# Two integer weight matrices handed to the kernel as bf16 instead of int32, read by the same casting-queue DMAs

## The chip, the cores and the metric

The kernel runs on 8 cores of one Trainium2 chip, one sequence of 2048 tokens on each core; no core exchanges anything with another. The metric is the time on the device of the slowest core, in microseconds (us).

## The reference, cut to what matters

```python
# x: (8, 2048, 1024); xn: layer norm of x
def _dequant(q, scales, g):            # q: integers 0..255, one scale per 128 rows and column
    K, N = q.shape
    w = (q.astype(float32) - 128.0).reshape(K // g, g, N) * scales[:, None, :]
    return w.reshape(K, N)
# layer 0, FFN
w1 = _dequant(fc1_q, fc1_scales, 128)  # fc1_q: int (1024, 4096)
y  = silu(h @ w1 + fc1_bias)
w2 = _dequant(fc2_q, fc2_scales, 128)  # fc2_q: int (4096, 1024)
z  = y @ w2 + fc2_bias
x  = x + attention0(xn) + (xn + 0.5 * z)
# layer 1: x = x + causal attention (16 heads) + FFN with values rounded to a small float format
```

The softmax of layer 0's attention runs over an axis of length one, so that attention is a sum of the values over all tokens and costs little. The change touches fc1_q and fc2_q alone.

## The kernel before, in words

The tokens of a core stay in SBUF as `X` (8 MB, f32). The program is a row of phases, each written as blocks for each engine; semaphores order the engines, and each instruction of VectorE and ScalarE waits for the one before on its engine (class `_Chained`, lines 56 to 97, so most rows carry L97 of that helper, and their waits L78).

The phases in order:

1. `_ph_loads` and `_ph_consts`: SP loads `X` and eight small tables (CON, a table of constants, is the last); VectorE makes constants once all of them are there.
2. `_ph_w1_dequant` (L430 to L464), eight rounds, one for each 128 rows g of fc1. POOL's queue loads `QIB` (128x4096, bf16 in SBUF) from `fc1q` (L439); ACT's queue loads `SCB` (128x2048 f32, one row broadcast to 128 partitions, 1 MB) for each half of the columns. For each half VectorE computes (QIB - 128) * SCB into `WB`, the whole of w1 in bf16 (8 MB). There is one QIB and one SCB: the next QIB is issued when both halves of the round are through (semaphore sDQ), the next SCB when the half before it is.
3. `_ph_w2_dequant_spill` (L467 to L514), 32 tiles of 128 rows of fc2. POOL's queue loads QIB (128x1024, two places used in turn) from `fc2q` (L480), ACT's queue loads SCB (128x1024 f32, 512 KB), VectorE computes the product into `WQB` (one place, 256 KB), and POOL's queue stores WQB to `w2sp` in HBM (L485). Product g waits for QIB g, SCB g and for the store of tile g-1 to have landed. When product g-1 is done, three DMAs go out: SCB g on ACT's queue, then on POOL's the store of tile g-1 and the load of QIB g+1, which is not needed until one tile later.
4. `_ph_ln` (layer norm statistics), `_ph_xsum_a0` (layer 0's attention), `_ph_ffn` for layer 0 with WB held and w2 streamed from `w2sp`; within it the tiles of layer 1's w2 are rounded on VectorE and stored to `wqsp`. Then the same for layer 1 (w1 loaded by `_ph_w1_load_l1`), the attention of layer 1, the projection and the store of `X`.

VectorE takes the phases in program order: the layer norm of phase 4 begins on it only when the products of phases 2 and 3 are through, and TensorE's first matmul waits for the layer norm's first pass.

QIB is a bf16 tile in SBUF. The sources are declared at L118 and L120 and prepared on the host at L1464 and L1466:

```python
c.fc1q = dram("fc1q", [D, FF], I32)
e.dma_start(out=c.QIB[:, :], in_=c.fc1q[128 * g:128 * (g + 1), :])     # L439
e.dma_start(out=c.QIB[:, D * (g % 2):D * (g % 2) + D],                 # L480
            in_=c.fc2q[128 * g:128 * (g + 1), :])
```

so these DMAs read 4 bytes an element, cast, and write 2. A row of fc1q is 16 KB in HBM and 8 KB in SBUF, a row of fc2q 4 KB and 2 KB.

Of the kernel before, what the change touches and what calls it, by code (L numbers as in the profile page):

```python
# [9 lines left out]
BF16 = mybir.dt.bfloat16  # L10
I32 = mybir.dt.int32
# [5 lines left out]
D = 1024  # L17
T = 2048
FF = 4096
# [86 lines left out]
def build_nc(stop="full"):  # L106
    _INC_REC.clear()
    _SEM_TOT.clear()
    nc = bass.Bass("TRN2", target_bir_lowering=False)
    c = Ctx()  # L110
    c.nc = nc
    c.stop = stop

    dram = lambda n, sh, ty, kind="ExternalInput": nc.dram_tensor(n, sh, ty, kind=kind).ap()
    c.x = dram("x", [128, NCH * T], F32)
    c.wvt = dram("wvt", [D, D], F32)
    c.wot = dram("wot", [D, D], F32)
    c.fc1q = dram("fc1q", [D, FF], I32)  # L118
    c.fc1sb = dram("fc1sb", [1, 8 * FF], F32)
    c.fc2q = dram("fc2q", [FF, D], I32)  # L120
    c.fc2sb = dram("fc2sb", [1, 32 * D], F32)
    c.gam = dram("gam", [128, NCH], F32)
    c.bet = dram("bet", [128, NCH], F32)
    c.f1b = dram("f1b", [128, NFO], F32)
    c.f2b = dram("f2b", [128, NCH], F32)
    c.qkvt = dram("qkvt", [D, 3 * D], F32)
    c.projt = dram("projt", [D, D], F32)
    c.bpj = dram("bpj", [128, NCH], F32)
    c.w1t = dram("w1t", [D, FF], F32)
    c.b1l1 = dram("b1l1", [128, NFO], F32)  # L130
    c.w2t = dram("w2t", [FF, D], F32)
    c.b2l1 = dram("b2l1", [128, NCH], F32)
    c.cvec = dram("cvec", [128, 8], F32)
    c.m4 = dram("m4", [128, 4 * TSW], BF16)
    c.out = dram("out", [128, NCH * T], F32, "ExternalOutput")
    c.w2sp = dram("w2sp", [FF, D], BF16, "Internal")
    c.wqsp = dram("wqsp", [FF, D], BF16, "Internal")
    c.rowsp = dram("rowsp", [4, T], F32, "Internal")
    c.rowspb = dram("rowspb", [1, D], BF16, "Internal")
    c.qksp = dram("qksp", [128, 2 * NCH * T], BF16, "Internal")  # L140
    c.f1sp = dram("f1sp", [128, NCH * T], F32, "Internal")

    with contextlib.ExitStack() as es:
        _body(c, es)
    return nc
# [1305 lines left out]
def host_prep(L0_attn_x, L0_attn_w_qkv, L0_attn_w_o, L0_ffn_ln_gamma,  # L1451
              L0_ffn_ln_beta, L0_ffn_fc1_q, L0_ffn_fc1_scales, L0_ffn_fc1_bias,
              L0_ffn_fc2_q, L0_ffn_fc2_scales, L0_ffn_fc2_bias, L1_attn_w_qkv,
              L1_attn_w_proj, L1_attn_b_proj, L1_ffn_w1, L1_ffn_b1, L1_ffn_w2,
              L1_ffn_b2):
    import ml_dtypes
    A = lambda v: np.ascontiguousarray(v)
    f32 = np.float32
    cm = lambda vec, k: A(np.asarray(vec, f32).reshape(k, 128).T)

    sh = {}
    sh["wvt"] = A(np.asarray(L0_attn_w_qkv, f32)[2048:3072, :].T)
    sh["wot"] = A(np.asarray(L0_attn_w_o, f32).T)
    sh["fc1q"] = A(np.asarray(L0_ffn_fc1_q, np.int32))  # L1464
    sh["fc1sb"] = A(np.asarray(L0_ffn_fc1_scales, f32).reshape(1, 8 * FF))
    sh["fc2q"] = A(np.asarray(L0_ffn_fc2_q, np.int32))  # L1466
    sh["fc2sb"] = A(np.asarray(L0_ffn_fc2_scales, f32).reshape(1, 32 * D))
    sh["gam"] = cm(L0_ffn_ln_gamma, NCH)
    sh["bet"] = cm(L0_ffn_ln_beta, NCH)
    sh["f1b"] = cm(L0_ffn_fc1_bias, NFO)  # L1470
    sh["f2b"] = cm(L0_ffn_fc2_bias, NCH)
    wq = np.asarray(L1_attn_w_qkv, f32)
    qkv = np.concatenate([wq[:, 0:64, :].reshape(NH * 64, D),
                          wq[:, 64:128, :].reshape(NH * 64, D),
                          wq[:, 128:192, :].reshape(NH * 64, D)], axis=0)
    sh["qkvt"] = A(qkv.T)
    sh["projt"] = A(np.asarray(L1_attn_w_proj, f32).T)
    sh["bpj"] = cm(L1_attn_b_proj, NCH)
    sh["w1t"] = A(np.asarray(L1_ffn_w1, f32).T)
    sh["b1l1"] = cm(L1_ffn_b1, NFO)  # L1480
    sh["w2t"] = A(np.asarray(L1_ffn_w2, f32).T)
    sh["b2l1"] = cm(L1_ffn_b2, NCH)
    cvec = np.zeros((128, 8), f32)
    cvec[:, 0] = 0.5 + 2.0 ** -20
    cvec[:, 1] = EPS
    sh["cvec"] = cvec
    p = np.arange(128)[:, None]
    qq = np.arange(TSW)[None, :]
    sh["m4"] = A(np.concatenate([(qq >= 128 * r + p) for r in range(4)],
                                axis=1).astype(ml_dtypes.bfloat16))  # L1490
    x = np.asarray(L0_attn_x, f32)
    in_maps = []
    for b in range(x.shape[0]):
        m = dict(sh)
        m["x"] = A(x[b].T.reshape(NCH, 128, T).transpose(1, 0, 2
                                                         ).reshape(128, NCH * T))
        in_maps.append(m)
    return in_maps
# [21 lines left out]
```

How the kernel before makes its waits and increments, by code:

```python
    def wait_ge(self, sem, val):  # L65
        return self._eng.wait_ge(sem, val)
# [1 line left out]
    def _edge(self):  # L68
        if self._prev is None:
            return
        rec = _INC_REC.get(id(self._prev))
        if rec is None or rec[1] is not self._seq:
            if rec is None:
                tgt = self._prev
            elif self._nop is not None:
                tgt = self._nop(self._eng)
            else:
                tgt = self._eng.engine_nop()
            _rec_then_inc(tgt, self._seq, 1)
            rec = _INC_REC[id(tgt)]
        self._eng.wait_ge(rec[1], rec[2])
# [287 lines left out]
    @blk.vector  # L369
    def _(e):
        e.wait_ge(c.sINd.h, c.sINd.v)
        e.wait_ge(c.sME.h, 1)
        e.tensor_scalar(out=c.CON[:, 2:3], in0=c.CON[:, 0:1], scalar1=C52,
                        scalar2=C52, op0=ALU.add, op1=ALU.subtract)
# [25 lines left out]
    @blk.gpsimd  # L400
    def _(e):
        for g in range(34):
            if g >= 2:
                e.wait_ge(c.sWQ.h, wq0 + g - 1)
            if g < 32:
                sb_ = c.sSPe if g % 2 == 0 else c.sSPo
                e.dma_start(out=c.SCW[:, 1024 * (g % 2):1024 * (g % 2) + D],
                            in_=c.w2t[128 * g:128 * (g + 1), :]
                            ).then_inc(sb_.h, 16); sb_.v += 16
            if g >= 2:
                e.dma_start(out=c.wqsp[128 * (g - 2):128 * (g - 1), :],
                            in_=c.WQB[:, :]
                            ).then_inc(c.sWQd.h, 16); c.sWQd.v += 16
# [860 lines left out]
    @blk.tensor  # L1274
    def _(e):
        e.wait_ge(c.sVTe.h, c.sVTe.v)
```

## Time and profile before

| | us |
|---|---|
| median of two runs | 4875.44 (4867.91 and 4882.96) |
| the profiled execution, its own time | 4875.03 |
| its span on the slowest core (core 7) | 4873.5 |
| spans of all cores | 4840.0 to 4873.5 |

The profiled execution's own time is 1.5 us more than its span, from the first to the last instruction. All cores show a mean granted TensorE clock of 0.669 to 0.672. The page names engines PE (TensorE), PEld (its weight loads), DVE (VectorE), ACT (ScalarE), POOL (GpSimd) and SP (SyncE); a "q" behind a name is its sequencer or queue. A DMA's bytes are counted as it writes them, so a load of QIB counts 1 MB or 256 KB whatever its source holds. DMA queues: q0 is POOL's, q10 ACT's, q1 SP's.

### The profile page before, as it was taken

Reading aid. Unit: us, or ns where it says so; the run is one execution under the profiler, and the core shown is the slowest. Engines: PE = TensorE matmul, PEld = TensorE weight load, DVE = VectorE, ACT = ScalarE, POOL = GpSimd, SP = SyncE. Lnnn points to the kernel's source line nnn. Section 1 sums busy time; section 2 is a strip of 40 time slices with the busy share of each in tenths; the row PEclk is TensorE's granted clock in tenths of the full one; section 3 lists DMA queues with packets and bytes.
Section 4 is the critical chain, followed back from the end, with each engine's and each line's share of the span. In section 5 each row is a group of like instructions: output and inputs, shape, how many; then the busy total and the mean of one; then the engine's idle time right before and its main releaser. Section 6 shows DMA issues by size and latency. Waiting matters only on the chain.

```text
span 4873.5 us, 25503 instructions; the slowest of 8 cores (4840.0 to 4873.5 us)
## 1 busy us (share of the span) xinstructions
PE 2228.2 (46%) x6689; PEld 726.5 (15%) x6689; DVE 1901.3 (39%) x2583; ACT 804.4 (17%) x1324; POOL 178.1 (4%) x336
## 2 busy tenths in 40 slices
PE   0002016384574246046145334423433577777775
PEld 0000002131231012012011111211110111111111
DVE  1213315555555373574466367333412111111113
ACT  0000003123130010010011011011000244444440
POOL 0010000000000000000000000000100000000001
PEclk9998558696886567566656765766755555555557
DMA  6563422231415202001100200223222100000005
GB/s 173 151 153 77 9 53 61 70 113 35 108 63 110 13 0 66 25 0 36 55 0 6 78 7 0 69 53 59 50 33 30 30 9 9 9 9 9 9 1 155
DMA packets 111755, 243.53 MB, mean 50 GB/s; under 512 B 31352, under 2 KB 35448, under 8 KB 107258
## 3 DMA queue, kind: packets, MB, share of 16 engines
q0 software_dynamic: 36112, 107.50, 9.8%
q1 hardware_dynamic: 57646, 85.12, 7.0%
q10 hardware_dynamic: 17856, 49.29, 4.3%
q8 instruction: 56, 0.92, 0.1%
q14 instruction: 85, 0.70, 0.1%
HBM read 243.89 MB, written 42.02 MB: 59 GB/s over the span
## 4 chain that ended last, share of the span: by engine, by line
DVE 37%; DMA 22%; PE 18%; ACT 10%; issue 9%; DVEq 2%; ACTq 0%; POOL 0%; SPq 0%; POOLq 0%
DVE SCR L97 26%; PE PS L1319 6%; ACT PT L97 6%; DVE YA L97 3%; PE PS L954 3%; DMA w2sp<-WQB 3%; DMA BCA<-rowsp 3%; DMA wqsp<-WQB 3%; PE PS L1298 2%; PE PS L1210 2%; DMA VW<-qkvt 2%; ACT SCR L97 2%; DMA W2B<-wqsp 2%; PE PS L1137 2%; DVE PT L97 2%
## 5 line engine op out<-in xcount | busy, mean ns | idle before, releaser
L890 PE MATMUL PS<-HBB,WB 128*128 128x512 bf16 x2048 | 668.2, 497 | 1081.0 <-DVE YA L97 429.2
L97 DVE TENSOR_TENSOR SCR<-SCR 128x512 f32<-128x512 f32 (+2 forms) x835 | 627.4, 751 | 442.3 <-DVEq L78 357.3
L954 PE MATMUL PS<-YA,W2B 128*128 128x512 bf16 x2048 | 469.6, 387 | 98.3 <-DVE YA L97 42.3
L890 PEld LDWEIGHTS PS<-HBB,WB 128*128 128x128 bf16 x2048 | 231.0, 117 | 1517.4 <-issue 1398.7
L200 ACT COPY CON<-CON 128x1 f32<-128x1 f32 x610 | 116.6, 191 | 1636.4 <-DVE YA L97 742.4
L1298 PE MATMUL PS<-PT,VT 128*65 128x512 bf16 x640 | 304.8, 631 | 143.4 <-DVE PT L97 143.4
L1319 PE MATMUL PS<-QKP 64*128 64x512 bf16 x640 | 299.3, 620 | 61.1 <-ACT PT L97 45.9
L97 DVE TENSOR_TENSOR SCR<-X,BCA 128x512 f32<-128x512 f32 x224 | 155.0, 692 | 404.1 <-DVEq L78 387.4
L97 ACT ACTIVATE PT<-PS 128x2048 bf16<-128x2048 f32 x160 | 300.4, 1877 | 14.8 <-ACT CON L200 0.5
L546 PE MATMUL PS<-YA,ONE 128*1 128x512 bf16 x64 | 39.3, 614 | 517.2 <-DVE YA L97 517.2
L954 PEld LDWEIGHTS PS<-YA,W2B 128*128 128x128 bf16 x2048 | 196.8, 99 | 372.8 <-issue 162.5
L1137 PE MATMUL PS<-XNS,QKW 128*128 128x512 bf16 x512 | 127.7, 416 | 249.9 <-DVEq L97 249.9
L97 DVE TENSOR_TENSOR PT<-PT,M 128x2048 bf16<-128x2048 bf16 x64 | 78.4, 1225 | 407.8 <-DVEq L78 405.9
L1210 PE MATMUL PS<-VW,XNS 128*128 128x512 bf16 x256 | 112.5, 618 | 201.9 <-DMA VW<-qkvt 129.0
L97 ACT ACT_TABLE_LOAD x10 | 12.8, 1283 | 1121.2 <-DVE STAT L97 498.0
L200 ACT ACT_TABLE_LOAD x23 | 29.5, 1283 | 986.8 <-PE PS L954 276.2
L97 DVE TENSOR_SCALAR SCR<-SCR,CON 128x512 f32<-128x512 f32 x320 | 165.1, 516 | 34.8 <-DVE SCR L97 0.5
L97 DVE TENSOR_SCALAR SCR<-SCR 128x512 f32<-128x512 f32 (+2 forms) x193 | 90.7, 470 | 191.5 <-DVEq L78 184.6
L1298 PEld LDWEIGHTS PS<-PT,VT 128*65 128x65 bf16 x640 | 87.2, 161 | 369.2 <-issue 369.2
L1282 PE MATMUL PS<-SCR,ONE 1*64 1x512 f32 x128 | 123.8, 1068 | 13.5 <-issue 10.2
L97 DVE TENSOR_TENSOR YA<-YA,PS 64x512 bf16<-64x512 bf16 x64 | 43.6, 681 | 208.0 <-DVEq L78 208.0
L97 DVE CAST YA<-PS 64x512 bf16<-64x512 f32 (+1 forms) x65 | 45.0, 692 | 189.1 <-DVEq L78 189.1
(83 smaller groups left out, 1551.2 us busy)
## 6 DMA issues: line engine op xcount, KB each, us to landing
W2B<-w2sp SPq DMA_DIRECT2D x64, 512.0 KB, 4.3
W2B<-wqsp SPq DMA_DIRECT2D x64, 512.0 KB, 3.5
SCB<-fc1sb ACTq DMA_DIRECT2D x16, 1024.0 KB, 5.8
SCB<-fc2sb ACTq DMA_DIRECT2D x32, 512.0 KB, 4.4
SCW<-w2t POOLq DMA_DIRECT2D x32, 512.0 KB, 4.6
BCA<-rowsp ACTq DMA_DIRECT2D x44, 256.0 KB
QIB<-fc1q POOLq DMA_DIRECT2D x8, 1024.0 KB, 10.4
QIB<-fc2q POOLq DMA_DIRECT2D x32, 256.0 KB, 5.7
```

Source lines behind the costliest of these rows:

```text
L97: ins = f(*a, **k)
L200: nop = lambda eng: eng.copy(out=c.CON[:, 7:8], in_=c.CON[:, 7:8])
L546: e.matmul(c.PS[0:1, sl], c.ONE[:, :], xb[:, sl], start=(g == 0), stop=(g == NCH - 1))
L890: mm = e.matmul(pb, c.WB[:, FF * g + 128 * fo:FF * g + 128 * (fo + 1)], c.HBB[:, TSW * g:TSW * (g + 1)], start=(g == 0), stop=(g == NCH - 1))
L954: mm = e.matmul(c.PS[:, 512 * d:512 * (d + 1)], c.W2B[:, off + 128 * d:off + 128 * (d + 1)], c.YA[:, TSW * g2:TSW * (g2 + 1)], start=(g2 = ...
L1137: mm = e.matmul(pb, c.QKW[:, 1024 * g + 128 * pc:1024 * g + 128 * (pc + 1)], c.XNS[:, TSW * g:TSW * (g + 1)], start=(g == 0), stop=(g == N ...
L1210: mm = e.matmul(c.PS[:, 1024 * tt + 512 * h2:1024 * tt + 512 * (h2 + 1)], st, c.VW[:, 512 * h2:512 * (h2 + 1)], start=(g == 0), stop=(g == ...
L1282: e.matmul(c.PS[0:64, nmb(hs2):nmb(hs2) + 512], c.ONE64[:, :], rrb(hs2), start=True, stop=True).then_inc(c.sPVt.h, 1)
L1298: e.matmul(c.PS[0:65, pvb(hs):pvb(hs) + 512], c.VT[:, 1040 * j + 65 * h:1040 * j + 65 * (h + 1)], c.PT[:, 2048 * (k % 2) + 512 * u: 2048 * ...
L1319: e.matmul(c.PS[:, 512 * u:512 * (u + 1)], c.QKP[prow, b + T + 128 * j:b + T + 128 * (j + 1)], c.QKP[prow, b + TSW * s:b + TSW * (s + 1)], ...
```

## The change

The two matrices are declared as bf16 in HBM and the host prepares them as bf16 (the integers 0 to 255 are exact in bf16). Everything else stays: the same DMAs on the same queues, the same waits, the same tiles, the same instructions in the same order on all engines. The DMAs of L439 and L480 now read 2 bytes an element and cast nothing; a row of fc1q is 8 KB and one of fc2q 2 KB in HBM, as in SBUF.

```diff
--- before
+++ after
@@ -115,9 +115,9 @@
-    c.fc1q = dram("fc1q", [D, FF], I32)
+    c.fc1q = dram("fc1q", [D, FF], BF16)
     c.fc1sb = dram("fc1sb", [1, 8 * FF], F32)
-    c.fc2q = dram("fc2q", [FF, D], I32)
+    c.fc2q = dram("fc2q", [FF, D], BF16)
     c.fc2sb = dram("fc2sb", [1, 32 * D], F32)
@@ -1461,9 +1461,9 @@
-    sh["fc1q"] = A(np.asarray(L0_ffn_fc1_q, np.int32))
+    sh["fc1q"] = A(np.asarray(L0_ffn_fc1_q).astype(ml_dtypes.bfloat16))
     sh["fc1sb"] = A(np.asarray(L0_ffn_fc1_scales, f32).reshape(1, 8 * FF))
-    sh["fc2q"] = A(np.asarray(L0_ffn_fc2_q, np.int32))
+    sh["fc2q"] = A(np.asarray(L0_ffn_fc2_q).astype(ml_dtypes.bfloat16))
```

## Rows read from the trace of the kernel before

**Rows 1.** The page: busy time of engines, and the chain that ended last.

```profile
PE 2228.2 (46%) x6689; PEld 726.5 (15%) x6689; DVE 1901.3 (39%) x2583; ACT 804.4 (17%) x1324; POOL 178.1 (4%) x336
...
DVE 37%; DMA 22%; PE 18%; ACT 10%; issue 9%; DVEq 2%; ACTq 0%; POOL 0%; SPq 0%; POOLq 0%
```

**Rows 2.** The chain in order of time, 0 to 425 us: start us, us, what.

```profile
5.87 36.44 DMA CON<-cvec
47.51 2.30 DVE WB L97
...
100.00 2.30 DVE WB L97
102.83 10.36 DMA QIB<-fc1q
113.48 2.30 DVE WB L97
115.85 4.61 DMA SCB<-fc1sb
120.67 2.30 DVE WB L97
123.50 10.49 DMA QIB<-fc1q
...
206.50 6.30 DMA QIB<-fc2q
...
301.99 4.32 DMA w2sp<-WQB
...
363.15 5.91 DMA w2sp<-WQB
...
424.14 1.24 DVE YA L97
```

**Rows 3.** The chain by line, 213.1 to 422.8 us.

```profile
by line: DMA w2sp<-WQB 70.2%; DVE WQB L97 18.3%; issue 10.1%; DVEq L78 0.4%; DVEq L81 0.3%; DVEq L66 0.3%; POOLq L484 0.3%; POOLq L478 0.2%
```

**Rows 4.** DMA queues, one round, 102.4 to 113.4 us: packets, MB, share of 16 engines.

```profile
q0 software_dynamic: 144, 1.05, 45.9%
q10 hardware_dynamic: 144, 1.05, 32.5%
```

**Rows 5.** DMA queues, 115.8 to 120.6 us, the second SCB of the round alone.

```profile
q10 hardware_dynamic: 144, 1.05, 57.4%
...
SCB<-fc1sb ACTq DMA_DIRECT2D x1, 1024.0 KB, 4.6
```

**Rows 6.** DMA queues, 0 to 42 us.

```profile
q1 hardware_dynamic: 1296, 8.45, 67.3%
q0 software_dynamic: 144, 1.05, 14.7%
q10 hardware_dynamic: 144, 1.05, 7.1%
```

**Rows 7.** DMA queues, 206 to 213.2 us, the first loads of fc2.

```profile
q0 software_dynamic: 284, 0.52, 40.9%
```

**Rows 8.** DMA issues, 206 to 424 us: KB each, median us to landing.

```profile
SCB<-fc2sb ACTq DMA_DIRECT2D x32, 512.0 KB, 4.4
QIB<-fc2q POOLq DMA_DIRECT2D x32, 256.0 KB, 5.7
w2sp<-WQB POOLq DMA_DIRECT2D x31, 256.0 KB, 4.6
```

**Rows 9.** DMA queues, 3818 to 3840 us: bf16 to bf16 loads on POOL's queue.

```profile
q0 software_dynamic: 720, 2.62, 38.5%
```

**Rows 10.** The page, DMA issues of the whole span: other stores of 256 KB.

```profile
wqsp<-WQB POOLq DMA_DIRECT2D x32, 256.0 KB, 4.7
...
f1sp<-SCR POOLq DMA_DIRECT2D x32, 256.0 KB, 2.3
```

**Rows 11.** The page, DMA queues and HBM traffic of the whole span.

```profile
q0 software_dynamic: 36112, 107.50, 9.8%
...
HBM read 243.89 MB, written 42.02 MB: 59 GB/s over the span
```

## The prediction, made before the changed kernel ran

> **What bounds the kernel now.** I read the page first, then the chain in order of time, then the DMA queues of single stretches. The page shows that no engine is full: PE is busy 46% of the span and DVE 39%, and the chain that ended last is DVE for 37%, DMA for 22% and PE for 18% [rows 1]. So the kernel hands work from engine to engine, and a transfer is worth something only where the chain waits for it. The chain in order of time shows where the change's transfers are. From 5.87 us it waits 36.44 us for the opening loads; then come the rounds of fc1, of which one reads: load of QIB 10.36, product 2.30, load of SCB 4.61, product 2.30, next load of QIB at 123.50, that is 20.67 us after the last one's 102.83 [rows 2]. Seven of the eight loads of fc1 stand so on the chain; the eighth (the first) lies in the opening. Next 6.30 us for the first load of fc2 at 206.50, and then the tiles of fc2, in which the load does not appear at all: 70.2% of 209.7 us is the store w2sp<-WQB [rows 3], 147.2 us over 31 stores, 4.75 us each, of which the shortest and the longest are 4.32 and 5.91 [rows 2]. At 424.14 us the layer norm starts on DVE right behind, so what these phases save moves everything after them. After that point nothing of the change is left. At most 424 us of 4873 are in play.
>
> **The change part by part.**
>
> *What a packet costs.* In a round's window of 11.0 us q0 carries 128 data packets of 8 KB as written (and 16 small ones) in 45.9% of 16 engines: 11.0 x 16 x 0.459 = 80.8 us, 0.63 us each [rows 4]. The same size uncast, SCB on q10, alone: 4.8 x 16 x 0.574 = 44.1 us for 128, 0.34 us each [rows 5]; beside QIB it is 11.0 x 16 x 0.325 / 128 = 0.45 us [rows 4]. So a cast packet, which reads 16 KB and writes 8, costs nearly twice an uncast one; the row says that the read side sets it (or the cast, which goes too).
>
> The Trainium skill ("DMA: Bandwidth & Descriptors", section on the anatomy of one DMA on the SWDGE path) fits a DMA as about 2.0 us plus bytes over 436 GB/s. With the bytes written it gives 4.4 us for a load of fc1 before and after, and a change of nothing; with the bytes read, 6.8 and 4.4, 2.4 us a load. Rows 4 and 5 bear out the second reading in size, since equal written bytes take 0.63 against 0.34 us.
>
> *Opening.* Over 42 us the queues fill 67.3 + 14.7 + 7.1 = 89.1% of all 16 engines, so the opening is bound by the DMA engines. The QIB packets take 42 x 16 x 0.147 / 128 = 0.77 us, those of SCB 42 x 16 x 0.071 / 128 = 0.37 [rows 6]. Eight packets an engine: 8 x (0.77 - 0.37) = 3.2 us saved. Bounds: 0 (if X's rate is set elsewhere) and 6.2 (all of the QIB packets).
>
> *Seven rounds of fc1.* QIB and the first SCB of a round go out together and both are needed. Eight packets an engine: 8 x 0.63 = 5.0 us before, 8 x 0.34 = 2.8 after, 2.3 us less. SCB's own packets were stretched by 0.45 - 0.34 = 0.1 us beside the 16 KB reads, 0.8 us in all; I take a good third of that back, 0.3 us. So QIB lands after 7.8 us instead of 10.4 and a round takes 18.1 us: 7 x 2.6 = 18.2 us. The product (2.30) and the second SCB (4.61) stay. Bounds: below, the uncast packets as dear as SCB's beside QIB, 8 x (0.63 - 0.45) = 1.4 us, 10 us in all; above, QIB lands no later than SCB does, 4.61 to 4.9 us, when SCB takes its place as the last: 5.7 x 7 = 40 us.
>
> *First loads of fc2.* Two loads go out back to back, 256 data packets at 7.2 x 16 x 0.409 / 256 = 0.18 us, 2.9 us an engine [rows 7]. Plain bf16 loads on the same queue with 4 KB packets take 22 x 16 x 0.385 / 640 = 0.21 us, with other loads queued [rows 9]. If POOL's queue puts two rows of 2 KB in a packet, as in the stores of WQB, that is 128 packets and 1.5 to 1.7 us an engine. Saved 1.4; bounds 0 and 1.9, when SCB's 4.4 [rows 8] is last (6.30 - 4.4).
>
> *31 tiles of fc2.* The load is issued behind the store on the same queue and is needed one tile later; now it lands in 5.7 us of a period of 6.76 [rows 3, 8]. The wait is for the store. What the load can give is less crowding of the store and of SCB: its engine time falls from 8 x 0.18 = 1.5 to about 4 x 0.2 = 0.8 us a tile. The nearest row is wqsp<-WQB, the same store beside a plain 512 KB load, with a median of 4.7 [rows 10], against 4.6 here [rows 8]; so the median need not move at all. The mean, 4.75, lies above the median by its longer cases up to 5.91, and I let these shrink: 0.2 us a tile, 31 x 0.2 = 6.2 us. Bounds: above, SCB (issued 0.5 us earlier, 4.4 us) becomes the last wait, which ends some 3.9 us after the store's issue: 0.85 x 31 = 26 us (a store with an empty machine takes 2.3 [rows 10], so the store itself would allow it); below, every store as long as the longest, (5.91 - 4.75) x 31 = 36 us lost.
>
> *POOL, DVE, PE, ACT.* No instruction is added, removed or moved on any engine, and QIB has the same type in SBUF, so products keep 2.30 and 1.24 us. After 424 us the phases shift as they stand.
>
> *Sum.* 3.2 + 18.2 + 1.4 + 6.2 = 29.0 us. From the profiled execution's own time, 4875.0 (0.4 under the median of the runs, 4875.4): 4846.0 us. That is 0.6%; about 2% is what a measurement of this kernel can tell from no change, which would be 97 us.
>
> **The rivals.**
>
> A. *SCB takes over.* With QIB cheap, the broadcast of SCB is the last to land in rounds and tiles, and the saving stops at SCB. For it: SCB is there after 4.61 alone, and q0's packets start on a free machine. Against it: both share the same 16 engines and QIB is still a full megabyte. Upper bounds together: about 3.2 + 40 + 1.9 + 26 = 71 us at the utmost; at two thirds, 4828.
>
> B. *The transfer is not faster.* The written bytes or the other cores' traffic in HBM set the pace: all eight cores read the same phases at once. For it: the opening moves 8.45 + 1.05 + 1.05 MB in 42 us at 89% busy engines, 251 GB/s as written, and each packet of q0 is already stretched from 0.63 to 0.77 [rows 4, 6]. Then only the lower bound of fc1 remains: 10 us, 4865. Against it: rows 4 and 5.
>
> C. *The tiles of fc2 get slower.* The load, with packets of two rows, now reaches the 16 engines together with the store it follows, and delays it or SCB at each tile. For it: the stores vary between 4.32 and 5.91 with the same work [rows 2], so their neighbours matter, and the load's data now come twice as fast. Against it: the load is behind the store in the same queue and has fewer packet-microseconds. Price if each store took the longest seen: +36 - 22.8 (the other three terms) = +13, 4888; it ends slower than before once a store takes more than 4.75 + 22.8 / 31 = 5.49 us in the mean.
>
> D. *Nothing carries over.* The shift of 29 us after 424 us is eaten by later waits. The chain is unbroken there [rows 2] and every load of the next phases is issued by an event of DVE or PE, so I give it little; it would end at 4875 less a few.
>
> **How the numbers follow.** The forecast's case (a saving of 15 to 45 us) has 0.74, A 0.09, B and D together 0.11, C 0.06. For each, 2% is far: the largest saving that the bounds allow is 73 us and the largest loss 13. So: same 0.97, faster 0.02 and slower 0.01, left for a bound that is wrong. Range: the upper end takes in B and the 7 us by which the two runs stand off their median, 4865 + 8 = 4873; the lower end is the forecast with the fc1 term at 30, the tiles at 17 and the other terms as they are, 4875 - 52 = 4823, and 7 us of scatter, 4816. C and the far half of A stay outside.
>
> **What would show it.** HBM read falls by 16.8 MB, from 243.9 to 227.1 [rows 11], whatever the time. Packets of q0 fall from 36112 by 32 x 64 = 2048 if two rows share a packet. In the chain, QIB<-fc1q reads 7.8 us (A: it vanishes in favour of SCB at 4.6 to 5; B: 9 or more); the first wait is 33 us instead of 36.4; the first load of fc2 is issued at 206.5 - 3.2 - 18.2 = 185 us and lands in 4.9; the stores average 4.55 (C: 5.5 or more); the layer norm starts at 395 instead of 424. If it does start there and the end comes no earlier, the steps hold and D is the error. The forecast is wrong if QIB's landing stays near 10 or if stores move by more than half a microsecond.

## The result, and the profile after

The changed kernel takes 4837.99 us (median of 15 runs, 4825.11 to 4859.99), the kernel before 4872.56 us over the runs taken beside it (median of 13). The ratio is 0.9926, with a 95% interval of 0.9902 to 0.9949: 0.5 to 1.0% faster, 34.6 us between the medians (25 to 48 by the interval). By the prediction's line of 2% that is "the same", as forecast. Forecast were 4846.0 us, a gain of 29.0, in a range of 4816 to 4873.

The profiled execution of the changed kernel took 4855.7 us, with a span of 4854.0 us on core 4. Since in some executions the cores of one die show a lower granted clock and end later, every median and ratio here leaves out those in which the difference is large, and the profiled execution of the changed kernel (die 1 at 0.661 against 0.669) is read only before TensorE begins. These are the page's rows that answer to [rows 8, 10, 11]:

```profile
DMA packets 109707, 243.53 MB, mean 50 GB/s; under 512 B 31352, under 2 KB 35448, under 8 KB 105210
...
q0 software_dynamic: 34064, 107.50, 8.8%
...
HBM read 227.11 MB, written 42.02 MB: 55 GB/s over the span
...
SCB<-fc1sb ACTq DMA_DIRECT2D x16, 1024.0 KB, 4.8
SCB<-fc2sb ACTq DMA_DIRECT2D x32, 512.0 KB, 4.3
...
QIB<-fc1q POOLq DMA_DIRECT2D x8, 1024.0 KB, 7.1
QIB<-fc2q POOLq DMA_DIRECT2D x32, 256.0 KB, 4.6
```

HBM read fell by 16.8 MB to 227.11, as worked out, and q0's packets by 2048 to 34064: where nothing is cast, the queue puts two rows of 2 KB in a packet.

The chain of the changed kernel in order of time (start us, us, what) answers to [rows 2]:

```profile
6.19 32.88 DMA CON<-cvec
44.28 2.30 DVE WB L97
...
109.19 7.27 DMA QIB<-fc1q
116.75 2.30 DVE WB L97
119.12 4.56 DMA SCB<-fc1sb
123.90 2.30 DVE WB L97
126.75 6.86 DMA QIB<-fc1q
...
178.50 4.44 DMA QIB<-fc2q
...
282.06 4.18 DMA w2sp<-WQB
...
367.19 5.11 DMA w2sp<-WQB
...
386.68 1.24 DVE YA L97
```

Read it piece by piece against the old chain: the same transfers stand in the same order, nothing has taken another's place. The wait for the opening is 32.88 instead of 36.44 us, the two loads of QIB shown 7.3 and 6.9 instead of 10.4 (the mean of all seven is 7.17 instead of 10.66), the first load of fc2 4.44 instead of 6.30. The layer norm begins at 386.68 instead of 424.14. The tiles' store is still what they wait for (by line, 183.2 to 385.4 us, answering to [rows 3]):

```profile
by line: DMA w2sp<-WQB 69.1%; DVE WQB L97 19.0%; issue 10.9%; DVEq L78 0.4%; DVEq L81 0.3%; DVEq L66 0.3%; POOLq L484 0.3%; POOLq L478 0.2%
```

69.1% of 202.2 us over 31 stores is 4.51 us each, after 4.75.

Single cores differ by up to 9 us at the layer norm, so the stages are compared as means over the eight cores' traces of one execution each. The stages are: the start of the first product; from there to the issue of fc2's first load (rounds); from there to the first product of fc2; from there to the layer norm (tiles).

| mean of 8 cores, us | opening | rounds | first load of fc2 | tiles | layer norm starts |
|---|---|---|---|---|---|
| before | 47.0 | 157.2 | 6.1 | 210.6 | 420.9 |
| changed | 43.8 | 133.7 | 4.9 | 202.9 | 385.3 |
| gain | 3.2 | 23.5 | 1.2 | 7.7 | 35.6 |
| forecast | 3.2 | 18.2 | 1.4 | 6.2 | 29.0 |

The 35.6 us at the layer norm fit the 34.6 us between the two medians. That they agree so closely is luck, since the end is known only to 25 to 48 us.

### The profile page after: what moved, and what is told of

Read it like the earlier page. It is cut to its first block, busy times and chain, and to the rows that moved or that the text cites. A ratio compares the mean times of both kernels' runs of the same rounds, so it can differ in the third digit from the quotient of the medians.

```text
span 4854.0 us, 25399 instructions; the slowest of 8 cores (4824.9 to 4854.0 us)
## 1 busy us (share of the span) xinstructions
PE 2263.8 (47%) x6585; PEld 738.6 (15%) x6689; DVE 1901.6 (39%) x2583; ACT 804.3 (17%) x1324; POOL 178.6 (4%) x336
## 3 DMA queue, kind: packets, MB, share of 16 engines
q0 software_dynamic: 34064, 107.50, 8.8%
HBM read 227.11 MB, written 42.02 MB: 55 GB/s over the span
## 4 chain that ended last, share of the span: by engine, by line
DVE 30%; PE 27%; DMA 20%; ACT 11%; issue 8%; DVEq 1%; ACTq 0%; SPq 0%; POOL 0%; POOLq 0%
DVE SCR L97 21%; PE PS L954 7%; PE PS L1319 6%; ACT PT L97 6%; PE PS L890 5%; DVE YA L97 3%; DMA w2sp<-WQB 3%; DMA BCA<-rowsp 3%; PE PS L1298 2%; PE PS L1210 2%; DMA VW<-qkvt 2%; PE PS L1137 2%; DMA W2B<-w2sp 2%; ACT SCR L97 2%; DMA W2B<-wqsp 2%
## 5 line engine op out<-in xcount | busy, mean ns | idle before, releaser
L890 PE MATMUL PS<-HBB,WB 128*128 128x512 bf16 x2006 | 682.3, 510 | 1083.3 <-DVE YA L97 430.6
L954 PE MATMUL PS<-YA,W2B 128*128 128x512 bf16 x2008 | 492.1, 404 | 87.1 <-DVE YA L97 42.3
L1319 PE MATMUL PS<-QKP 64*128 64x512 bf16 x640 | 299.3, 620 | 60.5 <-ACT PT L97 45.8
L1282 PE MATMUL PS<-SCR,ONE 1*64 1x512 f32 x128 | 123.6, 1066 | 13.6 <-issue 10.4
```

The costliest lines, as they stand in the source:

```text
L890: mm = e.matmul(pb, c.WB[:, FF * g + 128 * fo:FF * g + 128 * (fo + 1)], c.HBB[:, TSW * g:TSW * (g + 1)], start=(g == 0), stop=(g == NCH - 1))
L954: mm = e.matmul(c.PS[:, 512 * d:512 * (d + 1)], c.W2B[:, off + 128 * d:off + 128 * (d + 1)], c.YA[:, TSW * g2:TSW * (g2 + 1)], start=(g2 = ...
L1282: e.matmul(c.PS[0:64, nmb(hs2):nmb(hs2) + 512], c.ONE64[:, :], rrb(hs2), start=True, stop=True).then_inc(c.sPVt.h, 1)
L1319: e.matmul(c.PS[:, 512 * u:512 * (u + 1)], c.QKP[prow, b + T + 128 * j:b + T + 128 * (j + 1)], c.QKP[prow, b + TSW * s:b + TSW * (s + 1)], ...
```

## The experiments

Theory: a transfer that stands on the chain costs its packets' time on the 16 DMA engines; the larger side of the DMA, read or written, sets a packet; and what is saved before the layer norm arrives at the end. Rivals: the cast costs by itself; the cores' common traffic in HBM sets the pace; the tiles' gain is scatter; later phases eat the gain.

**One matrix at a time.** In e1 only fc1q is bf16, in e2 only fc2q. Against the changed kernel, e1 has the first edit of the two and e2 the second (the host's preparation follows each):

```diff
-    c.fc2q = dram("fc2q", [FF, D], BF16)
+    c.fc2q = dram("fc2q", [FF, D], I32)
...
-    c.fc1q = dram("fc1q", [D, FF], BF16)
+    c.fc1q = dram("fc1q", [D, FF], I32)
```

> fc1q bf16, fc2q int32 as before. Theory (only a transfer on the chain counts, its packets' read bytes set its price): opening and rounds as in the changed kernel, first product at 44 us, QIB<-fc1q landing in 7.1 us, first load of fc2 issued at 178 to 180 us; first load of fc2 lands in 6.3 and the tiles take 211 us as before; layer norm starts at 394 to 396 on the slowest core, the end 28 us earlier than before (ratio 0.994). Rival (the tiles of fc2 gain because the cores' HBM traffic as a whole is lower or because the cores run in another phase to each other): the tiles also shorten, to 203, and the layer norm starts at 387.

> fc2q bf16, fc1q int32 as before. Theory (the load crowds store and SCB on the 16 engines): opening 47.5 and rounds of 20.7 us as before; first load of fc2 lands in 4.5 instead of 6.3; 31 tiles in 203 instead of 211 us, store landings 4.5 instead of 4.75 in the mean; layer norm starts 9 us earlier than before, the end 9 us earlier (ratio 0.998, not to be told from 1). Rival (the tiles' shorter time in the changed kernel is scatter between executions): 211 again.

| | opening | rounds | first load | tiles | layer norm | ratio to before |
|---|---|---|---|---|---|---|
| e1 (fc1q bf16) | 43.7 | 133.9 | 5.9 | 212.5 | 396.0 | 0.9933 (0.9899 to 0.9967) |
| e2 (fc2q bf16) | 46.8 | 158.0 | 5.0 | 203.0 | 412.8 | 0.9976 (0.9937 to 1.0015) |

Each matrix gives its own stages' gain and leaves the other's alone: 24.9 us at the layer norm for fc1q, 8.1 for fc2q, 33.0 of the 35.6 together. The two values of a stage that should agree lie within 2 us of each other, which I take as the error of such a mean; the 2.6 us that are missing from the sum are of that size. The tiles' gain is no scatter: 203.0 and 202.9 with bf16, 212.5 and 210.6 without. The ratios at the end have the right size but say no more than the sign for e1 and nothing for e2.

**A cast with fewer bytes (e3).** Both matrices as uint8: a cast remains, the read side is half of what is written.

```diff
-    c.fc1q = dram("fc1q", [D, FF], BF16)
+    c.fc1q = dram("fc1q", [D, FF], U8)
-    c.fc2q = dram("fc2q", [FF, D], BF16)
+    c.fc2q = dram("fc2q", [FF, D], U8)
```

> Both matrices as uint8 in HBM, cast to bf16 by the same DMAs: reads a quarter of the bytes of int32, writes the same. Theory A (the slower of the two sides sets a packet: 16 KB read before, 8 KB written now): packets of QIB on q0 take 0.31 us, QIB<-fc1q lands in 7.0, layer norm starts at 385 to 388 as in the changed kernel, ratio to it 1.000. Theory B (the cast itself, per element, sets the price): packets take 0.63 us, QIB lands in 10.4, layer norm at 418 to 424. Theory C (HBM traffic of the eight cores sets it): faster than the changed kernel, QIB below 6.5 us, layer norm below 380.

The chain of e3, and the DMA queues of its stretch 109 to 117 us, one load of QIB:

```profile
89.35 7.12 DMA QIB<-fc1q
...
107.08 6.84 DMA QIB<-fc1q
...
124.27 6.85 DMA QIB<-fc1q
```

```profile
q0 software_dynamic: 144, 1.05, 33.2%
```

That is 8.0 x 16 x 0.332 / 128 = 0.33 us for a packet of 8 KB as written, although it is cast. That is theory A: the cast costs next to nothing, and it is the bytes of the larger side that take the time. Mean stages are 42.7, 133.5, 4.9 and 200.3 us, the layer norm at 381.5, 3.8 us before the changed kernel: a little below theory A's 385 to 388 and above theory C's 380. The rounds, where a load takes most, are the changed kernel's (133.5 against 133.7), so halving the reads once more gave nothing there. The median is 4834 us and the ratio to before 0.9883 (0.9801 to 0.9964), not to be told from the changed kernel's. q0's packets are 36112 again (a cast keeps the rows of 2 KB apart), and the tiles are not slower for it: the gain of 7.7 us does not need the pairing of rows, and what both have in common against int32 is the shorter time on the DMA engines and the smaller reads from HBM; these two are not told apart in the tiles.

**The hardware queue (e4).** Without a cast SP can issue the loads of fc1.

```diff
-    @blk.gpsimd
+    @blk.sync
     def _(e):
         for g in range(NCH):
```

> The changed kernel with the eight loads of fc1 issued by SP's hardware queue instead of POOL's. Theory (QIB's data go behind SCB's on the 16 engines, and the sum of both, 5.4 us, is what is waited for): landing of the later of both unchanged within 0.3 us, rounds of 17.3 us as in the changed kernel. Rival (part of the 7.1 us is the software queue's start, which the hardware queue saves): the later of both lands 0.7 to 1 us earlier, seven rounds save 5 to 7 us.

Rounds took 137.3 us in the mean, 3.6 more than in the changed kernel, so the rival (a gain of 5 to 7) is out, and the theory's "no change" is missed on the other side. The page's issues and the chain of the slowest core show what differs:

```profile
SCB<-fc1sb ACTq DMA_DIRECT2D x16, 1024.0 KB, 6.2
...
QIB<-fc1q SPq DMA_DIRECT2D x8, 1024.0 KB, 7.4
```

```profile
104.79 7.19 DMA SCB<-fc1sb
...
114.57 4.67 DMA SCB<-fc1sb
...
121.83 7.87 DMA SCB<-fc1sb
```

The 6.2 us for SCB is the median of two kinds, those beside QIB (7.19 and 7.87) and those alone (4.67). By the traces' landings, over seven rounds of eight cores, SCB beside QIB lands in 8.1 us instead of 5.0 and QIB in 7.8 instead of 7.1: on this queue both transfers run through each other and end together. The later of the two lands 8.08 us after SCB's issue, where it was 7.55, and 0.53 us times seven rounds is the 3.6 us. QIB's packets of 8 KB are what got longer, 0.39 us in the mean on SP's queue against 0.31 on POOL's, while SCB's took 0.32 against 0.35. Why, this one execution does not tell.

**The load off the chain (e5 int32, e6 bf16).** A second place for QIB in fc1, in a stretch of YA that is not in use then. A load goes out one round earlier.

```diff
...
-            if g >= 1:
-                e.wait_ge(c.sDQ.h, dq0 + 2 * g)
-            e.dma_start(out=c.QIB[:, :], in_=c.fc1q[128 * g:128 * (g + 1), :]
-                        ).then_inc(c.sDQd.h, 16); c.sDQd.v += 16
+            if g >= 2:
+                e.wait_ge(c.sDQ.h, dq0 + 2 * (g - 1))
+            sb_ = c.sQIe if g % 2 == 0 else c.sQIo
+            dst = c.QIB[:, :] if g % 2 == 0 else c.YA[:, 0:FF]
+            e.dma_start(out=dst, in_=c.fc1q[128 * g:128 * (g + 1), :]
+                        ).then_inc(sb_.h, 16); sb_.v += 16
...
```

> The kernel before (int32) with two places for QIB in fc1: round g+1's load is issued when round g-1 is through, so it is off the chain. Theory (only its place on the chain makes the load dear): a round is product, SCB, product, SCB stretched by the load beside it: 2.3 + 4.6 + 2.3 + 5.9 + 1.0 = 16.1 us instead of 20.7; first product 4 to 5 us later (a second QIB in the opening); rounds (first product to the issue of fc2's first load, mean of cores) 125 us instead of 157; layer norm near 394 instead of 421. Rival (the 16 engines' time is the limit): rounds stay above 145.

> The same with bf16 sources. Theory: the change is worth less where the load is off the chain: rounds of 15.5 us (SCB beside QIB 5.3 instead of 5.9), so 120 us against 125; opening 5 us less than with int32 (two loads); tiles 8 us less; layer norm 19 us before that of the int32 version instead of 35.6. Rival (the change is worth the same wherever the load stands, because it is traffic that counts): 35 us again.

| | opening | rounds | first load | tiles | layer norm | median |
|---|---|---|---|---|---|---|
| e5, int32 | 53.0 | 132.0 | 5.8 | 210.3 | 401.1 | 4854.9 (1 run) |
| e6, bf16 | 46.6 | 119.8 | 4.8 | 202.5 | 373.7 | 4805.1 (1 run) |

The chain of e5 between its first product and the issue of fc2's first load, 52.6 to 181.1 us, has no load of QIB any more:

```profile
by line: DMA SCB<-fc1sb 67.6%; DVE WB L97 28.7%; issue 2.8%; DVEq L78 0.3%; DVEq L81 0.3%; DVEq L66 0.2%; ACTq L66 0.2%; POOLq L479 0.0%
```

The rounds of e6 came out as expected (119.8 against 120); those of e5 did not (132.0 against 125). With int32 the load left the chain, where it had stood with 7 x 10.66 = 75 us, and the rounds became only 25 us shorter. The waits for SCB took its place, stretched by the load beside them (SCB's median landing is 6.0 us in e5 and 5.3 in e6), and the opening paid 6 us for the second load. I had expected the sources to matter for 19 us here, the rival 35 again; they matter for 27.4 (6.4 opening, 12.2 rounds, 1.0, 7.8 tiles), halfway between the two, so neither reading holds alone. Taking a load off the chain does not take it off the engines.

**Everything one step ahead (e7 int32, e8 bf16).** In addition two places for SCB (the second in SCR, in fc2 in SCB's free half) and for WQB (in QIB's free part). The core of the change in fc2:

```diff
...
-            if g >= 1:
-                e.wait_ge(c.sW2d.h, wd0 + 16 * g)
-            e.scalar_tensor_tensor(out=c.WQB[:, :],
+            if g >= 2:
+                e.wait_ge((c.sW2d if g % 2 == 0 else c.sW2o).h, 16 * (g // 2))
+            e.scalar_tensor_tensor(out=(c.WQB[:, :] if g % 2 == 0 else c.QIB[:, 2 * D:3 * D]),
...
```

> The kernel before with two places for QIB, SCB and (in fc2) WQB: all loads and stores one step ahead. Theory (with the waits gone the engines' time or the loop of issue and landing binds): rounds of fc1 10.4 us (8 x 0.63 + 16 x 0.34 us of packets on each engine), tiles 4.0 us; mean times: rounds 80 to 90 instead of 157, tiles 120 to 130 instead of 211; layer norm at 260 to 275; the end 150 us earlier than before (ratio 0.967 to 0.970) if the shift carries over whole. Rival (later phases eat it): layer norm at 265, the end less than 100 us earlier.

> The same with bf16 sources. Theory: rounds 8.0 us (8 x 0.34 + 16 x 0.34), tiles 3.5 us; rounds 62 to 70 in all, tiles 105 to 112, layer norm at 225 to 240, the end about 190 us before the kernel before (ratio 0.960) and 30 to 35 us before the int32 version: the change is worth about as much here as in the changed kernel, now because the engines' time binds. Rival (landing times, not packets, bind): 15 us or less between the two.

**Four tiles ahead (e9 bf16, e10 int32, e11 uint8).** In fc2 four places for QIB and for SCB, the first loads issued in the last round of fc1. The second place of WQB lies in YA here, so half of the stores read w2sp<-YA. Against the version with two places:

```diff
...
+    scb = [c.SCB[:, 0:D], c.SCB[:, D:2 * D], c.SCR[:, 0:D], c.SCR[:, D:2 * D]]
...
+            if g >= 4:
+                e.wait_ge(c.sW2.h, w20 + g - 3)
-            e.dma_start(out=c.SCB[:, D * (g % 2):D * (g % 2) + D],
+            e.dma_start(out=scb[g % 4],
...
-            e.dma_start(out=c.QIB[:, D * (g % 2):D * (g % 2) + D],
+            e.dma_start(out=c.QIB[:, D * (g % 4):D * (g % 4) + D],
...
```

> As the bf16 version with two places, but in fc2 four places for QIB and for SCB (loads four tiles ahead, the first of them issued in the last round of fc1). Theory (in the two-place version the tiles still waited for QIB's landing, 4.5 us a tile at 72% busy DMA engines): the DMA engines fill to 90% or more and a tile takes 3.4 to 3.8 us; layer norm at 240 to 250 instead of 274; the end 25 to 30 us before the two-place version, ratio to the kernel before 0.964 to 0.967. Rival (the store's landing on the two places of WQB takes over): 4.3 us a tile or more, layer norm above 265.

> The same with int32 sources. Theory: its DMA engines were at 90% with two places already, so it gains little: tiles 5.0 us, layer norm at 310 to 320 instead of 327; the bf16 sources are then worth 65 to 75 us of the time to the layer norm, twice what they are in the changed kernel (35.6). Rival (int32 reads cost no more once latency is hidden): 45 us or less between the two.

> The same with uint8 sources. Theory (the written side sets a packet for uint8 as for bf16): layer norm within 6 us of the bf16 version, 240 to 250. Rival (with all engines full the cores' HBM reads bind, and halving them once more pays): more than 10 us earlier than with bf16.

| | opening | rounds | first load | tiles | layer norm | median us | ratio to before (95%) |
|---|---|---|---|---|---|---|---|
| e7, int32 | 53.0 | 100.9 | 7.8 | 165.3 | 327.0 | 4751.5 | 0.9753 (0.9695 to 0.9810) |
| e8, bf16 | 46.5 | 82.6 | 6.3 | 138.7 | 274.1 | 4716.8 | 0.9714 (0.9645 to 0.9783) |
| e10, int32 | 52.5 | 91.7 | 11.5 | 131.2 | 287.0 | 4725.0 | 0.9764 (0.9679 to 0.9849) |
| e9, bf16 | 46.0 | 72.6 | 10.8 | 113.7 | 243.1 | 4682.5 | 0.9646 (0.9577 to 0.9715) |
| e11, uint8 | 44.5 | 65.3 | 9.6 | 109.1 | 228.4 | 4660.5 | 0.9614 (0.9542 to 0.9687) |

(The kernel before had a median of 4864.9 us beside e7 and e8 and 4846.4 beside the last three; in these three the first load of fc2 starts within fc1's last round, so its column overlaps the rounds. The cores of e7 spread from 308 to 339 us at the layer norm, so of the two pairs e9 and e10 is the firmer one.)

My sizes for e7 and e8 were too good (rounds of 100.9 and 82.6 us instead of 80 to 90 and 62 to 70, tiles of 5.3 and 4.5 us instead of 4.0 and 3.5), and the sources were worth 52.9 us between them and not 30 to 35. The rival for e7, that later phases eat the gain, did not come: 94 us at the layer norm, and 92 to 148 at the end by the interval of the ratio. For e9 my sizes held (113.7 / 31 = 3.7 us, layer norm at 243), for e10 too bad (4.2 us instead of 5.0). The chain of e8 in order of time shows what held its tiles, one landing of QIB for every two tiles (8.73 us from one to the next, 4.4 a tile), as the theory for e9 has it:

```profile
192.31 6.05 DMA QIB<-fc2q
...
198.72 1.24 DVE QIB L97
...
201.04 7.00 DMA QIB<-fc2q
```

Its DMA engines were not full between 140 and 260 us (queue: packets, MB, share of 16 engines):

```profile
q10 hardware_dynamic: 3882, 14.14, 39.7%
q0 software_dynamic: 4316, 14.14, 33.8%
```

That is 73.5%. In e9, between 145 and 200 us, they stand at 85.7% on the slowest core (89 to 93% on the others), and in e10, between 165 and 260 us, at 98.8%, these two fences in that order (each without its small third row):

```profile
q10 hardware_dynamic: 2067, 7.54, 45.8%
q0 software_dynamic: 2318, 7.58, 39.6%
```

```profile
q0 software_dynamic: 4799, 11.17, 50.8%
q10 hardware_dynamic: 3127, 11.42, 47.9%
```

So with int32 the engines are the limit and with bf16 nearly so. On the chain of e9, 60 to 240 us, the store of WQB's second place is the last wait again:

```profile
by line: DMA w2sp<-YA 44.1%; DMA SCB<-fc1sb 27.7%; DVE YA L97 9.6%; DVE WB L97 7.7%; issue 5.9%; DMA SCB<-fc2sb 5.6%; DVEq L78 0.3%; DVEq L66 0.2%; DVEq L81 0.2%; ACTq L88 0.2%; POOLq L495 0.1%; ACTq L66 0.1%
```

So e9's rival is half right, the store took over, but at 3.7 us a tile and not at 4.3.

What int32 costs against bf16 at the layer norm is 35.6 us in the kernel as it is, 27.4 with only QIB ahead (e5, e6), 52.9 in e7 and e8, 43.9 in e9 and e10. I had forecast 65 to 75 for the last pair. By its number (45 or less) the rival wins; its reason, that the reads cost nothing more once landings are hidden, does not fit engines at 98.8%. My size failed on e10, whose engines at 98.8% still moved a tile in 4.2 us: I had drawn 5.0 from e7's share and time of a tile. The share was the mistake: 90% was that of core 2, one of the two fastest cores of e7 (91% between 175 and 300 us), while six of the eight stood at 73 to 80% and had room to fill.

e11 with uint8 reaches the layer norm 14.7 us before e9, against my 6: the theory that the written side alone counts fails once all engines are busy. The opening gives 1.5 of it, the rounds 7.3, the tiles 4.6. The packets show a little more. In the tiles a tile costs the DMA engines the same time with both sources (3.3 us in the mean of the cores), and they are only less idle in e11 (92 to 96% busy between 145 and 200 us). In the rounds QIB's packets take 0.33 us instead of 0.39, but SCB's too, whose bytes are the same, 0.37 instead of 0.41, so it is not QIB's own read side alone. Whether it is the HBM traffic of the cores together, as the rival said, these runs don't tell. At 4660.5 us in the median e11 is the fastest of all, 3.1 to 4.6% faster than the kernel before, though its interval overlaps e9's.

## Why the prediction was right, step by step

- *Only the chain's transfers count.* Right as to where most of it lies: the seven rounds and the opening gave 26.7 of 35.6 us, as e1 shows alone; the loads of fc2, the same bytes in all but with 31 of 32 off the chain, gave 8.9. As a rule it is too strong, and the prediction's own term for the tiles already went past it: 7.7 us came from loads that nothing waits for, and e5 and e6 kept 27.4 of 35.6 us with fc1's loads off the chain too.
- *Opening, 3.2 us.* Measured 3.2.
- *Rounds, 18.2 us.* Measured 23.5: the term that was mis-sized. On the slowest core a load of QIB on the chain lands in 7.17 us in the mean of seven, where before it was 10.66 (47.1% of the 158.5 us from 47.5 to 206.0, by the chain by line), and not in 7.8. Over seven rounds of eight cores the later of the pair, always QIB, landed 10.64 us after SCB's issue before and 7.55 after: 3.1 us a round, where I had 2.6. Most of it is QIB's packets, 0.65 us before and 0.31 after in the mean, 8 x (0.65 - 0.31) = 2.7 us, where I had 2.3: I had priced the uncast packet at the 0.34 of one SCB. The second SCB of a round, which I had left as it was, went from 4.98 to 4.71 us, 0.3 us a round that the sum had put at nothing. 7 x (3.1 + 0.3) is the measured 23.5 within rounding. One round of the changed kernel, 108.7 to 116.7 us:

```profile
q10 hardware_dynamic: 144, 1.05, 31.2%
q0 software_dynamic: 144, 1.05, 31.1%
```

  That is 8.0 x 16 x 0.31 / 128 = 0.31 us a packet on both queues. The prediction's reading of SCB, 0.45 us beside a cast load against 0.34 alone, does not hold. It compared two single landings, and other rounds show the opposite, the kernel before at 80.9 to 92 us and the changed kernel at 73.6 to 82, in that order:

```profile
q10 hardware_dynamic: 144, 1.05, 24.5%
```

```profile
q10 hardware_dynamic: 144, 1.05, 34.0%
```

  11.1 x 16 x 0.245 / 128 = 0.34 us before, 8.4 x 16 x 0.34 / 128 = 0.36 us after. Over the 56 rounds of all cores SCB's packets beside QIB took 0.38 us in the mean before and 0.35 after, so the stretch was 0.03 us and not 0.1. The 0.3 us that I took back for it was near the 0.4 that the landing gained beyond QIB's own packets, by luck.
- *First load of fc2, 1.4 us.* Measured 1.2.
- *Tiles, 6.2 us.* Measured 7.7, with 4.51 us for a store instead of 4.75. The median of the stores moved from 4.6 to 4.4, which I had left open; e2 shows that the gain belongs to fc2's loads, e3 that it does not come from pairing rows.
- *It carries over.* Right as far as the interval tells: 35.6 us at the layer norm, 25 to 48 at the end. The larger shifts say the same more firmly: e9 reaches the layer norm 178 us earlier and ends 164 us earlier (138 to 205 by the interval of its ratio).
- *Rival A* (SCB last) did not come: QIB lands over 2 us after SCB in the rounds. It came in e5 and e6, where QIB is loaded ahead. *Rival B* would have left QIB near 9. *Rival C* (slower tiles) went the other way in e2. *Rival D* has no time left to explain.
- *The bounds.* The prediction's largest saving and largest loss, 73 and 13 us, do not follow from its own bounds: these add up to 74, and to a loss of 26 where the opening and the first load save nothing and the rounds 10. Both are still far from 2%, so nothing hangs on it.
- *The formula of the Trainium skill.* With the bytes read, the fit of the Trainium skill ("DMA: Bandwidth & Descriptors", anatomy of one DMA) gave an estimate of 2.4 us a load, with the bytes written nothing. The traces have 3.1 (QIB's landing, 10.2 us before and 7.1 after in the mean), of which 2.7 are QIB's own packets, so the first reading is the nearer one, somewhat short; e3 shows that for a source smaller than the destination it is the written side. By these three sources the larger of the two sides is what goes into it.

## What to carry to other kernels

Price a load by the larger of its two sides and by the other transfer that it delays, and then ask where it stands: on the chain each microsecond of it counted here, behind it less, but not nothing (7.7 us in 31 tiles, with DMA engines 64% busy before). Take the price of a packet from many landings: one round's mean of SCB's packets lay anywhere from 0.31 to 0.45 us. With the DMA engines nearly full the rule of the larger side missed 15 us between bf16 and uint8 (e11). The change of a type on the host gave 0.7%; putting loads and stores ahead gave 2.4% with the old type and the same work (e10), and the smaller type was then still worth 27 to 53 us. When a load is moved off the chain, look at what runs beside it: here the broadcast of SCB held a larger share of the engines than the loads and stores together (45.8% against 39.6% in e9).

## What the runs showed of the hardware

- A cast in a DMA costs next to nothing by itself: 8 KB packets as written take 0.33 us from uint8, with a cast, and 0.31 us from bf16, without. From int32, whose packets read 16 KB, they take 0.63 us, twice the uncast 0.31.
- An 8 KB packet of SCB's broadcast takes 0.35 us in the mean in the changed kernel, alone as beside a load of QIB (56 landings each); 71% of those beside QIB take under 0.32 us, and 5% over 0.6. One landing alone had 0.35 (59.7% of 4.7 us, 119.1 to 123.8 us), one beside QIB 0.31: that difference is scatter.
- POOL's queue pairs rows of 2 KB only where nothing is cast: 36112 packets with int32 and with uint8, 34064 with bf16.
- Beside ACT's queue a load on POOL's queue has its data moved behind SCB's (in every round its first packet starts 0.3 to 1.0 us before SCB's last one ends; mean landings 5.0 and 7.1 us), one on SP's queue among them (8.1 and 7.8). The pair is done 0.5 us later for it.
- The mean granted clock of e9 is 0.656 to 0.660 against 0.669 to 0.672 before, though TensorE was no slower: the idle stretch before it starts, in which the granted clock is full (1.00), is some 178 us shorter, and from TensorE's first instruction to the end the mean is 0.64 in both (cores 0 and 4).
